# First attention as one stream of slots, with scores in one fp32r pass over parts stacked on 32 rows

## The reference

```python
def _L0_attn_ref(hidden_states, wq, bq, wk, bk, wv, bv, wo, bo):
    H = 256; NH = 32; HD = H // NH
    q = heads(hidden_states @ wq.T + bq)
    k = heads(hidden_states @ wk.T + bk)
    v = heads(hidden_states @ wv.T + bv)
    scores = jnp.einsum('bhqd,bhkd->bhqk', q, k) / np.sqrt(HD).astype(np.float32)
    causal = jnp.tril(jnp.ones((S, S), dtype=bool))
    scores = jnp.where(causal, scores, -jnp.inf)
    attn = jax.nn.softmax(scores, axis=-1)
    out = jnp.einsum('bhqk,bhkd->bhqd', attn, v)
    return out @ wo.T + bo
...
x = L0_attn_hidden_states                      # (8, 256, 256), float32
xn = _layernorm(x)
x = x + _L0_attn_ref(xn) * _silu(_L0_ffn_ref(xn))    # top 2 of 8 experts, and a shared one
xn = _layernorm(x)
x = x + _L1_attn_ref(xn) * _silu(_L1_ffn_ref(xn))    # another attention; top 4 of 16 experts
```

## Time and profile before

| | us |
|---|---|
| median of three runs | 1923.16 (1921.44 to 1923.25) |
| the profiled execution's own time | 1924.45 |
| span of its trace, first to last instruction | 1922.6 |
| PE busy | 1815.3 (94% of the span) |
| DVE busy | 1282.4 (67%) |
| ACT busy | 906.2 (47%) |
| POOL busy | 832.7 (43%) |

### The profile page before, as it was taken

The page is one execution under the profiler, slowest core; times in us unless marked ns, Lnnn a source line. Parts: engine busy times, 40 slices in busy tenths (PEclk is TensorE's granted clock), DMA queues, the critical chain, the costliest instruction groups (busy, mean ns, idle before and its releaser), DMA issues.

```text
span 1922.6 us, 34586 instructions
## 1 busy us (share of the span) xinstructions
PE 1815.3 (94%) x11822; PEld 1443.5 (75%) x11822; DVE 1282.4 (67%) x2811; ACT 906.2 (47%) x2978; POOL 832.7 (43%) x919
## 2 busy tenths in 40 slices
PE   6999999999987999999999999999999997999986
PEld 4767666767765887788888888888888886777754
DVE  5678787863457788888676766667667664444467
ACT  3657564753433444445454455544545543444422
POOL 2000000320056665565767767777676773000066
PEclk9899999999999999999999999999999998999999
DMA  9600000123342000000000000000000223333344
GB/s 345 231 1 2 1 1 1 59 90 112 90 158 94 1 1 12 1 6 1 15 20 14 19 16 14 19 14 11 25 11 22 77 78 136 106 108 107 105 132 123
DMA packets 75907, 114.29 MB, mean 59 GB/s; under 512 B 9505, under 2 KB 65953, under 8 KB 73089
## 3 DMA queue, kind: packets, MB, share of 16 engines
q1 hardware_dynamic: 66416, 86.38, 13.6%
q0 software_dynamic: 9216, 25.18, 4.0%
q10 hardware_dynamic: 144, 1.05, 0.1%
HBM read 64.86 MB, written 47.71 MB: 59 GB/s over the span
## 4 chain that ended last, share of the span: by engine, by line
PE 77%; DVE 10%; POOL 5%; issue 3%; ACT 3%; DMA 2%; POOLq 0%; DVEq 0%; SPq 0%; ACTq 0%
PE ps L1356 11%; PE ps L1371 9%; PE ps L1443 5%; PE ps L1889 5%; PE ps L1397 4%; PE ps L640 4%; PE ps L624 3%; PE ps L1385 3%; PE ps L1384 3%; PE ps L1383 3%; PE ps L902 2%; POOL work L2084 2%; PE ps L1378 2%; PE ps L1906 2%; PE ps L1908 2%
## 5 line engine op out<-in xcount | busy, mean ns | idle before, releaser
L1356 PE MATMUL ps<-work,weights 128*128 128x256 f32 x1024 | 248.3, 386 | 1.1 <-DVE work L1629 1.1
L1371 PE MATMUL ps<-split 128*128 128x512 f32 x768 | 227.8, 419 | 0.0
L1356 PEld LDWEIGHTS ps<-work,weights 128*128 128x128 f32 x1024 | 186.4, 191 | 22.1 <-DVE work L1629 1.3
L1771 POOL TENSOR_TENSOR work<-work,rope 128x512 f32<-128x512 f32 x128 | 164.5, 1286 | 53.1 <-ACT work L1544 53.0
L1777 POOL TENSOR_TENSOR work<-work 128x512 f32<-128x512 f32 x128 | 164.4, 1284 | 5.0
L502 POOL DMA_INDIRECT xg<-work x96 | 96.9, 1009 | 153.1 <-PE ps L630 140.2
L2084 POOL DMA_INDIRECT work<-yg,work x64 | 62.4, 975 | 227.1 <-DMA yg<-work 207.3
L742 ACT ACTIVATE work<-ps,work 128x128 f32<-128x128 f32 x256 | 95.4, 373 | 124.3 <-DVE work L841 117.4
L1371 PEld LDWEIGHTS ps<-split 128*128 128x128 f32 x768 | 130.9, 190 | 24.6
L780 DVE COPY work<-ps 128x384 f32<-128x384 f32 x256 | 130.0, 549 | 8.5 <-PE ps L640 8.4
L1443 PE MATMUL ps<-weights,work 128*128 128x256 f32 x512 | 124.0, 386 | 2.5 <-ACT work L1600 2.5
(11 more groups left out here) (236 smaller groups left out, 4508.8 us busy)
## 6 DMA issues: line engine op xcount, KB each, us to landing
work<-xg SPq DMA_DIRECT2D x118, 128.0 KB, 2.2
yg<-work SPq DMA_DIRECT2D x118, 128.0 KB, 1.7
xg<-work SPq DMA_DIRECT2D x6, 2048.0 KB, 17.8
weights<-in_w SPq DMA_DIRECT2D x8, 1024.0 KB, 9.4
weights<-in_f SPq DMA_DIRECT2D x8, 1024.0 KB, 5.1
weights<-in_f SPq DMA_DIRECT2D x1, 4864.0 KB, 16.0
work<-xn SPq DMA_DIRECT2D x32, 128.0 KB, 2.2
weights<-in_wo SPq DMA_DIRECT2D x1, 2048.0 KB, 8.6
```

The costliest lines, as they stand in the source:

```text
L1356: last = pe.matmul(ps[:, 2, which * SEQ:(which + 1) * SEQ], w1(h, (which * KC + kc) * P, P), xT[:, kc, :], start=kc == 0, stop=kc == KC - 1)
L1371: last = pe.matmul(ps[:, 3, :], x1_split[:, xp, kc, c * P:(c + 1) * P], w_vg[:, n % 2, wp, kc, :], start=i == 0, stop=i == KC * len(TERMS) ...
L1771: pool.tensor_tensor(qk[:, h % 4, :, :], raw[:, h % 2, :, :], rope[:, 0, :].unsqueeze(1).broadcast_to([P, 2, SEQ]), ALU.mult).then_inc(rot ...
```

## The change

**Scores.** Queries and keys are rounded to fp32r (an upper part) and the rest is kept as a lower part (`split_heads`). A head's 8 rows times two parts of the query times two parts of the key fill its 32 rows, so that one fp32r product of 32 rows sums all four products of parts. The copies with zeros (`kTm`, MASK) are gone. `layout` reorders the columns of the query and key weights so that heads lie as the stack wants them.

**Through DRAM.** The parts are stacked by DMA: `write_halves` writes each part twice into a DRAM tensor `heads_by_part` (4 transfers of 256 KB for each of 4 projections of a turn), and `load_stack` reads 256 KB for each pair of slots into a ring of 5 (RINGQ). The first turn's parts are split on DVE, those of later turns on POOL.

**One stream.** The slots of all turns are numbered through (0 to 127). The transposes of inverses, the output projection, the projections of the next turn, the values, the logits and the norm are placed after the scores of certain slots (`lower_bank`, `upper_bank`), and the work between turns is gone.

**DMA order.** The zero rows are written in 15 parts of up to 1 MB, one after each stack from stack 7 on; the experts of layer 0, the shared expert and the first weights of layer 1 are loaded in turn 2.

```diff
+ALL = TURNS * SLOTS
+RINGQ = 5
+PROJ = 2 * KC
+STACKS = PAIRS
+ZB = TILES // 2
...
+        def split_heads(eng, t, n):
+            index, ring = t * PROJ + n, n % 2
+            eng.wait_ge(full_ready.sem, full_ready.at(t, n + 1))
+            if index >= 2:
+                eng.wait_ge(halves_written[ring], 16 * 4 * (index // 2))
+            eng.tensor_copy(halves[:, ring, 0, :], full[:, ring, :]).then_inc(upper_ready.sem, 1)
+            eng.wait_ge(upper_ready.sem, upper_ready.at(t, n + 1))
+            eng.tensor_tensor(halves[:, ring, 1, :], full[:, ring, :], halves[:, ring, 0, :], ALU.subtract).then_inc(lower_ready.sem, 1)
...
+            def lower_bank(t, s):
+                if s == 20:
+                    turn_inverse(t, 0)
+                if s == 22:
+                    project(t, 0)
+                if s == 24 and t < TURNS - 1:
+                    pe.wait_ge(s0_ready.sem, s0_ready.at(t, 1))
+                    values(0)
+                if s == 26 and t == TURNS - 2:
+                    pe.wait_ge(v_ready.sem, v_ready.at(t + 1, HPQ))
+                    route0.pe_rank(pe, 6)
...
+                else:
+                    if s == 4:
+                        turn_inverse(t - 1, 1)
+                    if s == 6:
+                        project(t - 1, 1)
+                if s == 8 and t < TURNS:
...
                     values(1)
...
+                    if s == 12:
                         pe.wait_ge(norm0.xT_ready.sem, norm0.xT_ready.at(t + 1, 2))
-                        logits(t + 1)
...
+                        logits()
+                    if 13 <= s < 13 + PROJ:
+                        n = s - 13
+                        if n == 0:
+                            pe.wait_ge(lg0_copied.sem, lg0_copied.at(t + 1, 1))
+                        else:
+                            pe.wait_ge(full_ready.sem, full_ready.at(t + 1, n))
+                        heads(t + 1, n, 7)
...
-                heads = [(2 * (s % 2) + hh, qT[32 * r:32 * r + 32, mt, :], kTm[32 * r:32 * r + 32, j, mt, :])
+                heads = [(2 * (g % 2) + hh, stack[32 * r:32 * r + 32, n % RINGQ, 0, :], stack[32 * r:32 * r + 32, n % RINGQ, 1, :])
                          for hh, r in enumerate(rows)]
...
+            for n in range(PROJ):
+                heads(0, n, 2 + n)
+            values(0)
+            pe.wait_ge(consts_loaded, NCONST)
+            pe.wait_ge(bias_done, 5)
+            pe.wait_ge(pow_rows, 7)
+            for g in range(ALL + 8):
+                t, s = divmod(g, SLOTS)
+                if g < ALL:
+                    scores(g)
+                lower_bank(t, s)
+                upper_bank(t, s)
...
+            def write_halves(t, n):
+                which, mt, ring = n % 2, n // 2, n % 2
+                sp.wait_ge(lower_ready.sem, lower_ready.at(t, n + 1))
...
+                for a in range(2):
+                    for b in range(2):
+                        sp.dma_start(rows[a, b], halves[:, ring, (a, b)[which], :].bitcast(F32)).then_inc(halves_written[ring], 16)
+
+            def load_stack(n):
...
+                if n >= RINGQ:
+                    sp.wait_ge(scores_done.sem, scores_done.at(0, 4 * (n - RINGQ) + 4))
...
             norm0.act_all(act, 0)
+            act.wait_ge(bias_done, 1)
+            act_heads(act, 0, 0, 2)
+            act_heads(act, 0, 1, 3)
+            act_heads(act, 0, 2, 4)
+            act_heads(act, 0, 3, 5)
             act.wait_ge(bias_done, 7)
             act.wait_ge(pow_rows, 6)
             act.wait_ge(consts_loaded, NCONST)
             act.copy(tri_r[:, :], keep_w[:, 0:P])
             act.copy(s2_split[:, :], weights[0:RS, W0S:W0S + NH1 * M]).then_inc(s2_upper, 1)
```

More of the change, by code:

```diff
@@ L257, in build @@
         eps_row, eps_dk, zeros = minus_half[:, 16:32], minus_half[:, 32:32 + ST * 2], minus_half[:, 48:49]
-        kTm = carve("attention", HPQ, KC, CH)
-        qT = carve("attention", KC, CH)
+        stack = part(0, RINGQ, 2, SEQ)
+        halves = part(RINGQ * 2 * SEQ, 2, 2, CH)
+        FULL_AT = RINGQ * 2 * SEQ + 4 * CH
+        full = work[:, FULL_AT:FULL_AT + 2 * CH].rearrange("p (a n) -> p a n", a=2)
+        assert FULL_AT + 2 * CH <= SPLIT1
+        used["attention"] = SPLIT1
         oT0 = carve("attention", KC, CH)
@@ L563, in values, with logits @@
                 last.then_inc(v_done.sem, 1)
-            def logits(turn):
+            def logits():
                 for c in range(CT):
@@ L688, in pe_attention0 @@
-            for s in range(SLOTS + LAG + 1):
-                if s < SLOTS:
-                    scores(s)
-                    beside(s)
-                for hh in range(2):
-                    if LAG <= s < SLOTS + LAG:
-                        turn(s - LAG, hh)
-                if s > LAG and (s - LAG) % 2 == 0:
-                    pv(s - LAG - 2)
-            turn_inverse(0)
-            if t < TURNS - 1:
-                pe.wait_ge(probT_ready.sem, probT_ready.at(t, HEADS2))
-                pe_queries_keys(pe, t + 1, 0)
@@ L701, in pe_attention0 @@
[L701 to L713 removed]
+            pe.wait_ge(norm0.xT_ready.sem, norm0.xT_ready.at(0, KC))
@@ new lines, in act_heads, with act_attention0, values @@
+        def act_heads(act, t, n, bank):
+            which, mt = n % 2, n // 2
+            index = t * PROJ + n
+            act.wait_ge(proj_done.sem, proj_done.at(t, n + 1))
+            if index >= 2:
+                act.wait_ge(lower_ready.sem, lower_ready.at(0, index - 1))
+            act.activation(full[:, n % 2, :], ps[:, bank, :], ACT.Identity, bias=(bqs, BK)[which][:, mt:mt + 1],
+                           scale=(HD0 ** -0.5, 1.0)[which]).then_inc(full_ready.sem, 1)
+        def act_attention0(act):
+            def values(t, c):
@@ new lines, in act_attention0, with dve_attention0, copy_probs, inverse @@
+            values(0, 0)
+            for g in range(ALL + 4):
+                if g < ALL:
+                    exponentials(g)
+                beside(*divmod(g, SLOTS))
+        def dve_attention0(dve):
+            def copy_probs(g):
+                for hh in range(2):
+                    dve.wait_ge(prob_turned.sem, prob_turned.at(0, 2 * g + hh + 1))
+                    if g >= RINGT:
+                        dve.wait_ge(pv_done.sem, pv_done.at(0, 2 * (g - RINGT) + hh + 1))
+                    dve.tensor_copy(probT[:, g % RINGT, hh, :], ps[:, 4 + hh, 0:BLK]).then_inc(probT_ready.sem, 1)
+            def inverse(t, bb):
@@ L2230, in _ @@
                 norm0.pool_all(pool, t)
+                for n in range(PROJ):
+                    split_heads(pool, t, n)
             pool.wait_ge(xg_zeroed, 16 * ZERO_PARTS)
@@ L2269, in _ @@
             dve.tensor_copy(bias_wide, BV.unsqueeze(2).broadcast_to([P, KC, P])).then_inc(bias_ready0, 1)
+            for n in range(PROJ):
+                split_heads(dve, 0, n)
             dve.wait_ge(consts_loaded, NCONST)
```

436 lines of the change are left out of this document (214 added, 222 removed).

## The result

The changed kernel takes 1935.36 us in the median of 4 runs (1932.47 to 1937.54), the kernel before 1923.2 in the same comparison. The ratio is 1.0064 with an interval of 1.0046 to 1.0081: 12 us slower, where 20 us faster was forecast. The profiled execution took 1937.54 us, its span is 1935.7. Against the forecast's 1904.7 for that execution 32.8 us are missing. Two marks split them: the expert stage starts at 413.98, not at 399 (15.0), and the other 17.8 are lost behind it, where nothing had been changed.

What follows compares the result with a forecast made beforehand. PE bounds the attention at 2.31 us a slot, then DVE at 2.0. Start 40.8 + 1.1 + slots 256 + pieces 55 + 16.6 + 12 + clock 10.5 + tail 7.0 = 399, against 418.8: 1903.4 us, range 1890 to 1919, with rivals 1883 to 1925.

Steps and rivals of the forecast that it cites:

- other pieces and the clock: In the attention: PE and DVE pieces other than the inverses, plus time lost at half clock; 84.3 us together.
- behind the last maxima: Attention's tail: exponentials, transposes, last value product, inverse and output projection take 9.0 us from the last slot's maxima.
- Nothing behind the attention changes: Everything after the attention stays as before; weights now loading in turn 2 have 90 us of it and more.
- Pieces beside slots: Projections, inverses, values, norm, logits and router work placed in slots add 55 us on PE, 16.6 and 12 on DVE.
- The clock: Half clock while DMA moves 348 GB/s makes slots 3.3 us: 9.5 lost, 10.5 with products after a start wait.
- rival B: PE pauses in each DVE-paced slot, so its clock may fall outside the DMA stretch too: 1940 us; chance 0.10.
- The chain at the start: First scores wait for projection, DVE, transfers, ACT's casts, POOL's subtraction and memsets: 40.8 us instead of 27.1.
- the slots paced by DVE: DVE's round, not PE, sets each attention slot: 2.0 us for 128 slots, 256 us against 296.
- the fp32r price: Scores with bias in each slot take 0.6 us in one fp32r pass, against 1.08 before.
- no gap at turns: Sign: the attention's stream shows no gap at slots 32, 64, 96.
- rival C: Stacks come late, sharing one queue with zero rows and parts; at 150 GB/s the time is 1945 us; chance 0.04.
- Rival A: PE's pieces hide in its spare 0.26 us per slot: 1876 us if half hides, 1885 if a third; chance 0.20.

Runs made afterwards that it cites:

- Experiment 4: Idle PE instructions added to shift the loop's place: changed kernel with 194, 1921.67 us; kernel before with 62, 1938.51 us; other counts on the changed kernel too.
- experiment 2: Changed kernel with ACT's copy of the finished outputs ahead of the exponentials of slots 3 and 19: 1911.69 us, ratio 0.9936.
- experiment 3: Changed kernel with POOL's small memset of ones_b ahead of POOL's subtraction and large memset: ratio 1.0018.

## Why the prediction was wrong

The sum, term by term, against the trace of the changed kernel:

| term | forecast | measured |
|---|---|---|
| first scores | 40.8 | 43.0 |
| to first maxima | 1.1 | 1.3 |
| 127 slots between first and last maxima, at 2.0 | 254 | 263 (2.07) |
| pieces, inverses in seven slots | 9.8 | 26 |
| other pieces and the clock | 84.3 | 70.6 |
| behind the last maxima | 9.0 | 10.0 |
| expert stage starts | 399 | 414.0 |
| what follows, against before | 0 | +17.8 |

**The step "Nothing behind the attention changes" failed, and with it the sign.** The instructions and waits behind the attention are the same, and the trace of before has PE busy for 119.77 of 120 us in layer 1. But PE's code had become 962 instructions shorter ahead of a loop that was just kept, and the loop then fetched its code again in each later pass. It loses 4.7, 4.4, 4.4 and 2.7 us in the four later passes, 16.2 of the 17.8. Experiment 4 shows the cause from both sides: the kernel before, moved to the same place, loses 18.1 in these passes, and the changed kernel, moved away, nothing. With the loop at a fast place the changed kernel stands at 1921 (98 idle instructions, ratio 0.9987), within what counts as no change.

Another 1.3 us are lost in the first two pairs of layer 1, ahead of the loop, and not by its place: experiment 2 has the place and not the loss. There PE waits for POOL, and the clock fell behind the longer of the two waits. Changed kernel, then experiment 2:

```profile
628.12 2.76 PE L1434 MATMUL ps<-work 64*128 64x256 f32 x16 [2.88 <-POOL work L1814]
```
```profile
603.15 1.58 PE L1434 MATMUL ps<-work 64*128 64x256 f32 x16 [1.53 <-POOL work L1814]
```

**The step "Pieces beside slots" failed in one piece.** The inverse was priced by PE's 0.45 us and DVE's 0.95 in seven slots, 9.8 in all. What stands ahead of it was not followed: ACT's copy, behind two slots' exponentials. In the kernel before, PE turned the inverses in the drain only, where no slot waited behind them. Measured are 26 us beyond undisturbed slots (40.7 - 7 x 2.07), and 3.6 with the copy first. The order of ACT's list at slots 3 and 19 would have shown it; the prediction read it at the start only.

**The clock** was given 9.5 us for a reason that does not hold. The earlier trace rows show a low clock and full DMA together; experiment 2, and the kernel before from 52.7 to 62.7 us, have the full clock with the same DMA. The clock of the attention did fall (0.92, 0.97 before) and rival B was right in that much, though not for pauses in each slot but in large part for the long waits at L602. With these gone it is 0.96, and 1.00 from 67 to 223 us.

**What held.** The chain at the start, with each link; the slots paced by DVE (4.14 us a pair against 4.0); the fp32r price; no gap at turns; no scores waiting for a stack (rival C), the transfers moving 339 GB/s. Rival A had something: in experiment 2 a projection of the output adds 3.33 - 2.27 = 1.06 us to its slot and not 1.8. With the copies first, everything between first and last maxima takes 334.0 us where 348.1 were forecast. So two opposite errors stand in the forecast of the attention: the wait missed, worth 359.7 - 334.0 = 25.7 us, and the other pieces and the clock, priced 14 us too high; that the expert stage came only 15 us late is in part luck. The range reached to 1925 for rivals in the attention; no rival dealt with the rest of the program, and the measured time lies beyond it. Two small slips changed nothing: the bounds named for the forecast's own range add up to 1892 and 1921, not 1890 and 1919, and the transfers of rival C would have eaten the gain below 173 GB/s (24 MB in 118 + 20 us), not 179.

## What to carry to other kernels

A piece that moves into another stream brings along what it waits for: for each one, read the lists of all engines that feed it, at the new place. A change of an engine's instruction count moves every later loop against the blocks of 256 instructions in which its code is fetched: after such a change compare the fetches (queue "instruction") in the loops, and where they rise, try some idle instructions at a place where the engine waits anyway, before judging the change itself. Here 98 of them, an earlier memset and one moved copy turned +0.6% into -1.8%.

## What the runs showed of the hardware

A loop of 1740 PE instructions ran with at most one fetch from 1000 to 1480 us at the places 72, 168 and 200 modulo 256, and with 7 to 9 fetches of 16 KB in each 120 us at 222, 230, 22 and 32, for 3 to 10 us a pass. The Trainium skill (Trainium Architecture — The Big Picture, The software stack) says that the instruction streams are loaded when the program is loaded; the traces show fetches through the whole execution (75 packets in the kernel before, 107 in the changed one). An idle instruction of PE costs 0.106 us (97, 128 and 194 at the very start let the first product begin at 18.88, 22.04 and 29.14: 10.26 / 97), and about 0.08 ahead of the first scores (PE waits 18.47 us there with 226). In experiment 3 POOL's memset of 3.51 us ran beside the end of one of DVE's maxima (0.68 us, as elsewhere) and the norm's statistics (1.40 us, 1.39 without it): the slots take 359.8 us from first to last, 359.7 without it.
